# Attention-and-FFN sandwich kernel: first stack piece issued by two queues, second piece ahead of the weights, idle matmuls in the head

## The reference, cut to what matters

```python
# x: (8, 512, 256) float32; 16 heads of 16; 8 experts, LoRA rank 4, hidden 1024
def attn(x):
    q, k, v = split((x @ w_in.T + b_in).reshape(b, 512, 16, 48))
    att = softmax(einsum('blhd,bmhd->blmh', q, k) / 4, axis=2)       # over the keys m
    return einsum('blmh,blhd->blhd', att, v) @ w_out.T + b_out        # v of the query's own row
def ffn(x):
    top1 = argmax(softmax(x @ gate_W.T + gate_b))
    inter = relu(x @ wi_W.T + wi_b + (x @ lora_A[top1].T) @ lora_B[top1].T)
    return inter @ wo_W.T + wo_b
x = x + layernorm(attn(layernorm(x)))
x = x + layernorm(ffn(layernorm(x)))
```

## Time and profile before

| | |
|---|---|
| runs | 564.1, 564.52, 565.22 us |
| profiled execution, its span | 565.43 us, 563.6 us |
| TensorE busy | 508.8 us (90%) |
| VectorE busy | 480.3 us (85%) |
| ScalarE busy | 465.2 us (83%) |
| GpSimd busy | 215.3 us (38%) |
| chain that ended last | PE 60%, ACT 24%, DVE 7%, POOL 4%, DMA 2%, issue 2% |

### The profile page before, as it was taken

How to read it: one execution, slowest core, us unless ns; L and a number is a source line. 1 busy time by engine, 2 the same in 40 slices (tenths; PEclk the granted TensorE clock), 3 DMA queues, 4 the chain that set the end, 5 groups by cost and what they waited for, 6 DMA issues and landing times.

```text
span 563.6 us, 8533 instructions
## 1 busy us (share of the span) xinstructions
PE 508.8 (90%) x2640; PEld 406.8 (72%) x2640; DVE 480.3 (85%) x1021; ACT 465.2 (83%) x1254; POOL 215.3 (38%) x388
## 2 busy tenths in 40 slices
PE   2848997879999999999999999999999998899986
PEld 1625465638778877887788877887788767777875
DVE  5369989998999999989999999999998898828234
ACT  2369999999999998999899999999899988942230
POOL 8395013602360257114920295026701642163142
PEclk9979789888999999999999999999999998989998
DMA  6286352053404423232505341533133230010011
GB/s 238 86 215 170 90 135 76 1 149 76 113 0 105 114 64 94 64 97 66 151 4 146 76 111 39 141 86 74 37 92 98 66 85 1 2 34 4 1 38 37
DMA packets 22292, 46.16 MB, mean 82 GB/s; under 512 B 5109, under 2 KB 13429, under 8 KB 21624
## 3 DMA queue, kind: packets, MB, share of 16 engines
q1 hardware_dynamic: 21624, 44.77, 30.0%
q10 hardware_dynamic: 624, 0.85, 0.5%
HBM read 7.85 MB, written 4.19 MB: 21 GB/s over the span
## 4 chain that ended last, share of the span: by engine, by line
PE 60%; ACT 24%; DVE 7%; POOL 4%; DMA 2%; issue 2%; SPq 1%; ACTq 0%; POOLq 0%; DVEq 0%
PE pu L166 29%; ACT ps L380 17%; PE ps L183 15%; PE ps L166 5%; PE pu L232 5%; ACT inter L445 3%; DVE nmax L527 2%; PE pu L188 2%; DVE st L557 1%; ACT oT L408 1%; DMA stack<-qk 1%; ACT qk L394 1%; PE pu L274 1%; DVE inter L553 1%; POOL wo_r L810 1%
## 5 line engine op out<-in xcount | busy, mean ns | idle before, releaser
L380 ACT ACTIVATE ps<-ps,nmax 128x512 f32<-128x512 f32 x512 | 342.7, 687 | 12.0 <-DVE nmax L527 11.4
L527 DVE TENSOR_REDUCE nmax<-ps 128x1 f32<-128x512 f32 x512 | 320.8, 680 | 23.8 <-PE ps L183 22.9
L183 PE MATMUL ps<-stack 128*128 128x512 f32 x512 | 186.3, 445 | 30.7 <-ACT ps L380 26.1
L183 PEld LDWEIGHTS ps<-stack 128*128 128x128 f32 x512 | 93.6, 197 | 80.0 <-ACT ps L380 63.1
L380 ACT ACTIVATION_READ_ACCUMULATOR ps<-ps,nmax 128x1 f32 x512 | 119.7, 234 | 0.0
L166 PE MATMUL pu<-wo_r,inter 128*128 128x256 f32 x624 | 84.2, 285 | 0.0
L166 PEld LDWEIGHTS pu<-wo_r,inter 128*128 128x128 f32 x624 | 80.1, 190 | 3.6 <-DVE qk L541 1.0
L166 PE MATMUL pu<-yT,wi_r 128*128 128x512 f32 x312 | 81.6, 396 | 0.0
L762 POOL TENSOR_TENSOR ml<-gs,g 128x128 f32<-128x128 f32 x8 | 3.3, 414 | 168.1 <-DVE g L644 168.1
L166 PEld LDWEIGHTS pu<-yT,wi_r 128*128 128x128 f32 x312 | 58.3, 189 | 12.4
L166 PE MATMUL pu<-xnT,wqk_r 128*128 128x512 f32 x192 | 50.7, 411 | 1.9 <-DVE xnT L531 1.9
(11 more groups left out here) (117 smaller groups left out, 619.8 us busy)
## 6 DMA issues: line engine op xcount, KB each, us to landing
stack<-qk SPq DMA_DIRECT2D x248, 128.0 KB, 2.6
xb<-in_x SPq DMA_DIRECT2D x7, 512.0 KB, 3.7
out_y<-xb SPq DMA_DIRECT2D x7, 512.0 KB, 3.0
xb<-in_wo SPq DMA_DIRECT2D x1, 1024.0 KB, 7.9
vo<-in_wi SPq DMA_DIRECT2D x2, 512.0 KB, 7.1
stack<-qk SPq DMA_DIRECT2D x12, 64.0 KB, 2.0
xb<-in_x SPq DMA_DIRECT2D x4, 128.0 KB, 3.9
oT<-in_wqk ACTq DMA_DIRECT2D x1, 512.0 KB, 3.9
```

The lines of the kernel that those rows point to most:

```text
L183: e.matmul(ps[i % NS][:], st[:, 1 - p, c, t * 128:(t + 1) * 128], st[:, 2, c, :], start=True, stop=True).then_inc(scored, 1)
L380: e.activation(ps[i % NS][:], ps[i % NS][:], ACT.Exp, bias=nmax[:, i % 8:i % 8 + 1], accum_out=ssum[:, b % 2, t, h:h + 1]).then_inc(exped, 1)
L527: e.tensor_reduce(nmax[:, i % 8:i % 8 + 1], ps[i % NS][:], AX_X, ALU.max, negate=True).then_inc(maxed, 1)
```

## The change

`first_piece` gets one semaphore for each half (c, p) instead of one for each c, and TensorE waits for both. GpSimd, not ScalarE, issues (0, 1), and GpSimd, not SyncE, issues (1, 1); both stand ahead of GpSimd's weight work. SyncE issues piece 1 right behind (1, 0), ahead of its wait for `late` and of the weights. TensorE gets matmuls of `ones_r` by itself whose result nobody reads (`run_idle`): 25 before the transposes, 6 between transposes and projections, 4 ahead of pair 0, and one ahead of each score matmul of pairs 2 to 33, but for the eight pairs whose number less 2 stands in `FULL`: 24 pairs, 48 matmuls.

```diff
+IDLE, FULL = (25, 6, 4), (7, 8, 12, 13, 15, 27, 28, 30)
...
-        first_stacked = [sem(f"first_stacked{c}") for c in range(2)]
+        first_stacked = [[sem(f"first_stacked{c}_{p}") for p in range(2)] for c in range(2)]
...
-                            qk[p:128:8, qa:ka + 1:ka - qa, c].bitcast(F32)).then_inc(first_stacked[c], 16)
+                            qk[p:128:8, qa:ka + 1:ka - qa, c].bitcast(F32)).then_inc(first_stacked[c][p], 16)
...
+            def run_idle(bank, n):
+                for _ in range(n):
+                    e.matmul(bank[:].rearrange("p (k m) -> p k m", k=4), ones_r[:],
+                             ones_r[:].unsqueeze(1).to_broadcast([128, 4, 128]), start=True, stop=True)
...
                 if g in (0, 4):
-                    e.wait_ge(first_stacked[c], 128)
+                    e.wait_ge(first_stacked[c][0], 64)
+                    e.wait_ge(first_stacked[c][1], 64)
...
                     if i >= NS:
                         e.wait_ge(exped, i - NS + 1)
+                    if 2 <= g < PAIRS + 2 and g - 2 not in FULL:
+                        run_idle(ps[i % NS], 1)
...
+            e.wait_ge(const_set, 1)
+            run_idle(ps[0], IDLE[0])
             e.wait_ge(id_loaded, 16)
...
+            run_idle(ps[0], IDLE[1])
             e.wait_ge(qk_split, 3)
...
                 value(0, t)
+            run_idle(ps[0], IDLE[2])
             pair(0), pair(1)
...
             q_k(0, 0), q_k(0, 2)
-            first_piece(e, 0, 1)
             q_k(0, 1), q_k(0, 3)
...
-            e.wait_ge(qk_low, 4)
+            first_piece(e, 0, 1)
+            first_piece(e, 1, 1)
             late_halves(0, [(wi_r[:, :, 0, half(i)], wi_st[:, half(i)]) for i in range(2)], wi_loaded, 16)
...
             first_piece(e, 0, 0)
             first_piece(e, 1, 0)
-            first_piece(e, 1, 1)
+            stacks(0, 1)
             e.wait_ge(late, 4)
...
-            stacks(0, 1), stacks(0, 2)
+            stacks(0, 2)
```

## The result

| | before | changed |
|---|---|---|
| runs, median (lowest to highest) | 565.16 us (564.1 to 566.84), 8 runs | 560.68 us (557.3 to 562.11), 8 runs |
| span of the profiled execution | 563.6 us | 558.1 us |
| PE / DVE / ACT / POOL busy | 508.8 / 480.3 / 465.2 / 215.3 | 522.8 / 479.5 / 464.6 / 219.7 |

The changed kernel is faster: ratio 0.9911, 95% interval 0.9891 to 0.9932, that is 5.0 us (3.8 to 6.2); the medians differ by 4.5. The forecast was 561.3 us. By the intervals, two ratios that differ by less than about 0.003 (1.7 us) can't be told apart.

The account below looks back on a forecast made before the run. ScalarE's exponentials, 0.669 us per item, bound the kernel, so time comes only from reaching that pace sooner: 3.2 + 0.35 - 0.3 = 3.25 us off gives 562.2 us profiled, 561.3 median; range 557.8 to 564.7.

Parts of the forecast that it names:

- The head, clock: Before pair 0: idle matmuls end at 9.2, projections run 12.5 to 17.9, fourth evacuation ends 19.4, first exponential at 23.45.
- P, GpSimd's cost of an issue: First piece: each DMA issue by GpSimd costs 1.0 us; each 0.1 us on it moves the whole kernel by 0.8 us.
- The estimate of 0.99: First piece: GpSimd's issue cost from the Trainium skill's first-byte ratio, 0.594 x 1/0.6 = 0.99 us, near the 1.0 taken.
- The likeliest case: Whole kernel: a gain of 1.1 to 5 us, time 559.5 to 563.2 us; chance 0.43.
- the rival "as cheaply as SyncE": First piece: GpSimd issues at 0.594 us each, second four end 2.95 us earlier, gain 6.2, time 558.3 us; chance 0.24.
- The new wait in place of the old: Before the transposes behind pair 9: ScalarE stands about 3.7 us for GpSimd's x; item 20 at 42.6, 3.2 us earlier.
- The wait at item 10: ScalarE in batch 0: its 1.45 us wait stays, as VectorE's statistics for batch 1 stand there.
- Piece 1 and piece 3: ScalarE's waits for these pieces of the stack, 3.08 us before item 16 and 0.35 us at 53.45, both go.
- a sign of being wrong: Before pair 0: the prediction listed pair 0 waiting for the half that GpSimd issued; no size given.
- Idle matmuls in the pairs: Pairs 11 to 13 may run at the lower clock: loss at most 1.3 us, at least 0, taken as 0.3.
- 0 to 0.5: Later stretches: keeping the clock up buys little, taken as 0 us, at most 0.5.
- Carried on to the end: After batch 0: no later loss in the sum; in 62 to 75 ScalarE lost nothing with TensorE at clock 0.50.

## Why the prediction was right in its sum, and where its terms were not

- **The head, clock**: right. Idle matmuls ended at 9.0 (forecast 9.2), projections 12.44 to 18.15 (12.5 to 17.9), fourth evacuation ended at 19.66 (19.4), first exponential 23.38 (23.45).
- **P, GpSimd's cost of an issue**: the failed term. I took 1.0 us, from the nearest GpSimd row; it is 0.507 at the median, 0.53 over eight, below even the 0.594 that I had made its lower bound. The bound was wrong in kind: a SyncE row does not bound a GpSimd operation. So was the row taken: 0.953 mixed three shapes, and rows of 0.236 and 1.037 us on the same tile left everything between open. The estimate of 0.99 that stood beside it was off by as much. The likeliest case was the wrong one; the rival "as cheaply as SyncE" gave 2.95 us more at item 20, so 6.15, and the trace shows 6.4 us instead of 3.2.
- **The new wait in place of the old**: right in kind (TensorE 1.88 us, ScalarE 1.09 instead of 3.7). Of the 3.2 us that item 20 comes earlier than forecast, 2.8 are P; the other 0.4 are the transposes, which took 0.63 us at the upper clock where I had carried over the 1.05 of before. The delay by one memset moved item 20 by its own length and more, which confirms the path up to there; in time no loss was seen. The wait at item 10 was 0.88, not 1.45.
- **Piece 1 and piece 3**: right. No wait for piece 1, none for piece 3. In the run where SyncE issues all, it began piece 1 6.2 us later and piece 3 5.3 us later. Not foreseen: the landing of the first piece is no constant 2.0 to 2.4 us. In four later profiles SyncE's last DMA of the half for pair 0 landed 3.9 to 4.1 us after its issue began, and pair 0 waited for it, which the prediction had listed as a sign of being wrong.
- **Idle matmuls in the pairs**: 0.3 us of loss was too cautious for this run (the clock never fell in batch 0), and "0 to 0.5" for their later use is inside what the run without them leaves open: the ratios do not differ.
- **Carried on to the end**: the step that was missing. The forecast let a gain of batch 0 pass unchanged, since ScalarE had lost nothing at the lower clock in 62 to 75; but where ScalarE evacuates a dense group of TensorE's, it does lose (1.31 us at the gate's projection). In the two profiles of the changed kernel 1.6 and 2.9 us of it go between items 63 and 127, by the lower clock over the gate's projection and, once, the output projections. The forecast of 3.25 us was 3 us too low at item 30 (6.3), and the unforeseen loss took back half of that or more. That the sum came out near the measured 4.5 to 5.0, inside the band of the likeliest case, is luck: by its mechanism the run belongs to the rival with cheap issues, whose own time, 558.3, it missed for the same unforeseen loss.

The cause of the give-back is shown by the two kernels with idle matmuls in batch 1: their profiles have neither the low clock there nor the steps at items 80 and 112. In time each is 2.4 us below the same kernel without them, each alone within noise, both the same way. What sets the moment at which the clock falls was not settled: the changed kernel's two profiles differ in it.

## What to carry to other kernels

Many small transfers inside the chip, as here, cost mostly their issues: count them on each queue, and give part of them to an engine that is idle there. Time one issue on that engine first: no row of other work told its price. When a wait is removed, compute the next latest chain to its end and follow the gain past the changed stretch, since a later batch can give it back. Idle matmuls paid here where dense matmuls followed on which another engine waits (head and batch 1); in the pairs of batch 0 no gain could be measured.

## What the runs showed that I had not expected

GpSimd issues a 64 KB DMA in 0.507 us (0.743 for the first), faster than SyncE (0.594) and ScalarE (0.672). SyncE is also less regular: in ten of the eleven profiles of kernels other than before, one of its issues of the first piece or piece 1 took 1.2 to 1.9 us (one of 1.51 in the changed kernel), while no issue of GpSimd's took over 0.743. The row of granted clock gives 1.00 for the stretches before its first event: in the earlier trace rows the first 12 projection matmuls take 0.44 us each, the lower level, where the record still says nothing, so durations have to be read beside it.
